# Perceiver layer on one core: Wv and Wo of the last cross-attention group multiplied beforehand, and the end of cross-attention reordered

## The reference, cut to what matters

```
x = x + xattn(layernorm(x), ctx)     # 16 heads over 8 K/V groups; x is 2 x 128 x 256, ctx is 2 x 2048 x 128
x = x + attn(layernorm(x))           # causal, 16 query heads, 4 groups
x = x + ffn(layernorm(x))            # 16 routed experts, top 2, and one shared
def xattn(h, c):
    q = h @ Wq;  k = c @ Wk;  v = c @ Wv
    attn = softmax(q @ k.T / sqrt(128))
    return (attn @ v) @ Wo
```

## Time and profile before

| | us |
|---|---|
| median of 3 executions | 351.37 (351.33 to 351.54) |
| the profiled execution, its own time | 349.24 |
| its span in the trace | 347.5 |
| TensorE busy in the span | 331.4 (95%) |
| DVE, ACT, POOL busy | 271.0, 232.4, 236.1 |

### The profile page before, as it was taken

One profiled execution on the slowest core, in us unless ns is written; L12 is line 12 of the kernel. 1 busy time (PEld: TensorE's weight loads), 2 busy tenths in 40 slices (PEclk: granted clock), 3 DMA queues, 4 the chain that ended last, 5 costly groups with the idle time before them and its releaser, 6 DMA issues.

```text
span 347.5 us, 6872 instructions
## 1 busy us (share of the span) xinstructions
PE 331.4 (95%) x2246; PEld 299.8 (86%) x2246; DVE 271.0 (78%) x469; ACT 232.4 (67%) x415; POOL 236.1 (68%) x146
## 2 busy tenths in 40 slices
PE   6899989999999999999999998999899999999995
PEld 5788868898999999999999987999798897698995
DVE  3787788897988988989889887754559745579997
ACT  3789467667687687777767775975355686266761
POOL 4593728798599599499598596859626768507650
PEclk9999999999999999999999999999999999999999
DMA  6811468776886895895795887890232040404630
GB/s 199 249 32 38 100 153 189 196 176 152 220 189 144 204 204 127 208 208 125 178 204 117 201 181 183 208 321 31 87 101 83 2 151 1 144 9 124 179 107 31
DMA packets 32566, 49.98 MB, mean 144 GB/s; under 512 B 5537, under 2 KB 23073, under 8 KB 32545
## 3 DMA queue, kind: packets, MB, share of 16 engines
q1 hardware_dynamic: 32544, 49.72, 56.6%
HBM read 20.08 MB, written 0.26 MB: 59 GB/s over the span
## 4 chain that ended last, share of the span: by engine, by line
PE 71%; DVE 9%; POOL 6%; issue 4%; ACT 4%; SPq 3%; DMA 2%; DVEq 0%; POOLq 0%; ACTq 0%
PE bank L573 10%; PE pair L573 10%; PE bank L574 10%; PE bank L575 10%; PE pair L574 10%; PE pair L575 10%; POOL pT L431 4%; SPq L272 3%; PE bank L717 2%; PE bank L876 1%; DMA ctx_raw<-in_ctx_dram 1%; DVE ctx_raw L1495 1%; PE bank L709 1%; PE pair L869 1%; DMA pT<-blocks 1%
## 5 line engine op out<-in xcount | busy, mean ns | idle before, releaser
L431 POOL TENSOR_TENSOR pT<-pT,pT_hi 128x1024 fp32r<-128x1024 f32 x56 | 133.4, 2407 | 35.3 <-ACT pT_hi L1135 35.3
L1125 ACT ACTIVATE probs<-probs,lowest 128x2048 f32<-128x2048 f32 x32 | 64.3, 2009 | 26.5 <-DVE lowest L1484 26.4
L1135 ACT ACTIVATE pT_hi<-pT 128x1024 fp32r<-128x1024 f32 x56 | 57.6, 1053 | 16.1 <-DMA pT<-ctx_raw 10.5
L573 PE MATMUL bank<-pT_hi,ctx_lo 128*128 128x256 f32 x224 | 63.8, 285 | 0.4 <-POOL pT L431 0.4
L574 PE MATMUL bank<-pT,ctx_hi 128*128 128x256 f32 x224 | 64.1, 286 | 0.0
L575 PE MATMUL bank<-pT_hi,ctx_hi 128*128 128x256 f32 x224 | 63.6, 284 | 0.0
L573 PE MATMUL pair<-ctxT_hi,qk_lo 128*128 128x512 f32 x128 | 52.1, 407 | 2.4 <-DVE lowest L1484 2.0
L575 PE MATMUL pair<-ctxT_hi,qk_hi 128*128 128x512 f32 x128 | 50.1, 391 | 0.0
L574 PE MATMUL pair<-ctxT_lo,qk_hi 128*128 128x512 f32 x128 | 50.1, 391 | 0.0
L1484 DVE CUSTOM_DVE_ANT_0 probs<-pair,mask_bias,lowest 128x1024 f32<-128x1024 f32 x32 | 41.0, 1281 | 9.3 <-PE pair L575 8.5
L431 POOL TENSOR_TENSOR ctx_lo<-ctx_raw,ctx_hi 128x512 fp32r<-128x512 f32 (+1 forms) x19 | 31.5, 1671 | 21.8 <-DVE route L1817 9.4
(11 more groups left out here) (253 smaller groups left out, 841.3 us busy)
## 6 DMA issues: line engine op xcount, KB each, us to landing
pT<-blocks SPq DMA_DIRECT2D x112, 128.0 KB, 2.3
pT<-ctx_raw SPq DMA_DIRECT2D x112, 128.0 KB, 2.3
ctx_raw<-ffn_experts_gate_up_dram SPq DMA_DIRECT2D x16, 256.0 KB, 2.8
wq<-in_L_xattn_Wq_dram SPq DMA_DIRECT2D x8, 256.0 KB, 2.6
ctx_raw<-in_ctx_dram SPq DMA_DIRECT2D x8, 256.0 KB, 6.4
wo<-in_L_xattn_Wo_dram SPq DMA_DIRECT2D x8, 256.0 KB, 2.8
blocks<-in_L_attn_w_dense_dram SPq DMA_DIRECT2D x4, 512.0 KB, 4.6
ctx_raw<-_L_ffn_experts_down_dram SPq DMA_DIRECT2D x16, 128.0 KB, 2.4
```

Of the source, the lines that this page charges most:

```text
L431: pool.tensor_tensor(dst, src, hi.bitcast(F32), ALU.subtract).then_inc(ready, 1)
L573: pe.matmul(dst, w[1], x[0], start=start, stop=False)
L1125: act.activation(probs[:, j], probs[:, j], ACT.Exp, bias=lowest[:, p, j, 1:2], scale=-1.0, accum_out=den[:, p, j:j + 1]).then_inc(exps, 1)
L1135: act.activation(hi_slot(c), chunk(p, c).bitcast(F32), ACT.Copy).then_inc(pT_hi_ready, 1)
```

## The change

For the last group alone, y_project and its round trip are removed: Wv and Wo are multiplied with each other beforehand. TensorE transposes Wv (`v_turn`), ACT copies it into wk, TensorE multiplies it with both halves of Wo in one plain float32 matmul (`vo_product`), ACT rounds the product into wq_hi and DVE makes wq_lo; `vo_project` then takes o straight to the output. `o_round(7)` and `rest_o(7)` are gone.

Further: in the last group ACT's oT_unit stands ahead of the first two p_rounds. Of the last unit's four low parts POOL makes those of chunks 0 and 2, DVE those of 1 and 3 (`odd_rest`). The last unit's attention is cut in blocks (`attend_blocks`) and spread around vo_project(14) and the transposes of batch 0. ACT rounds the query weights before oT of unit 14, and splits xnT before oT of unit 15. `scores2(0, 0)` comes before the transposes of batch 1, with two warm-up matmuls on either side of these in place of one, and the first query of batch 1 begins with the matmuls that need only the high part (`first_query`).

```diff
                 beats(g, True)
             for g in range(G - 2, G):
                 beats(g, False)
-            rest_o(G - 1)
-            for c in range(4):
+            for c in (0, 2):
                 rest_p(LAST - 1, 0, c)
             def split_q(r):
...
                                    (hi_block(c, i), lo_block(p, blk)), blk == 0, blk == NBLK - 1)
                 last.then_inc(av, 1)
+            def attend_blocks(first, end):
+                dst = O_BANK[0].rearrange("p (j q t) -> p j q t", j=J, q=QD)
+                for blk in range(first, end):
+                    c, i = blk // 4, blk % 4
+                    if i == 0 and c % 2 == 0:
+                        pe.wait_ge(pT_lo_ready, 4 * (LAST - 2) + c // 2 + 1)
+                    if i == 0 and c % 2 == 1:
+                        pe.wait_ge(odd_lo_ready, c // 2 + 1)
+                    last = product(dst, (ctx_hi[:, 0, blk], ctx_lo[:, 0, blk]), (hi_block(c, i), lo_block(0, blk)),
+                                   blk == 0, blk == NBLK - 1)
+                    if i == 3:
+                        last.then_inc(av, 1)
             def y_project(n, g):
-                w = (wkT_hi, wkT_lo) if isinstance(g, int) and g == G - 1 else (wv_hi, wv_lo)
                 pe.wait_ge(wv_ready, g + 1)
                 pe.wait_ge(oT_ready, n + 1)
                 after(pe, added, 2 * n)
-                product(YO_BANK[:, 0:J * T], (w[0][:], w[1][:]), (oT_hi[:], oT_lo[:]),
+                product(YO_BANK[:, 0:J * T], (wv_hi[:], wv_lo[:]), (oT_hi[:], oT_lo[:]),
                         True, True).then_inc(y_psum, 1)
             def out_project(n, g):
-                w = (wq_hi, wq_lo) if isinstance(g, int) and g == G - 1 else (wo_hi, wo_lo)
                 pe.wait_ge(wo_ready, g + 1)
                 pe.wait_ge(yT_ready, n + 1)
                 for j in range(J):
                     rows = slice(j * T, (j + 1) * T)
                     last = product(YO_BANK[:, j * H:(j + 1) * H], (yT_hi[:, rows], yT_lo[:, rows]),
-                                   (w[0][:, j], w[1][:, j]), True, True)
+                                   (wo_hi[:, j], wo_lo[:, j]), True, True)
+                last.then_inc(out_psum, 1)
+            def v_turn():
+                pe.wait_ge(ld_wv, 16 * G)
+                pe.wait_ge(masked, NB)
+                pe.transpose(bank[2][:, 0:P], wv[:], ident[:]).then_inc(vo_psum, 1)
+            def vo_product():
+                pe.wait_ge(vT_ready, 1)
+                pe.wait_ge(ld_wo, 16 * G)
+                pe.matmul(bank[2][:], wk[:], wo[:].rearrange("p j n -> p (j n)"), start=True, stop=True
+                          ).then_inc(vo_psum, 1)
+            def vo_project(n):
+                pe.wait_ge(vo_ready, 1)
+                pe.wait_ge(oT_ready, n + 1)
+                pe.wait_ge(added, 2 * n)
+                for j in range(J):
+                    rows = slice(j * T, (j + 1) * T)
+                    last = product(YO_BANK[:, j * H:(j + 1) * H], (oT_hi[:, rows], oT_lo[:, rows]),
+                                   (wq_hi[:, j], wq_lo[:, j]), True, True)
                 last.then_inc(out_psum, 1)
             def beat(g, m, fold_on, out_on, y_on):
...
                 if h == 1:
                     last.then_inc(done, 1)
+            def first_query(head, cols):
+                dst, (_, hi, lo) = QA[:, cols], wq2_of[0]
+                at = [slice((k * HR + head) * P, (k * HR + head + 1) * P) for k in range(HB)]
+                for k in range(HB):
+                    pe.matmul(dst, lo[:, at[k]], xnT_hi[:, k, cols], start=(k == 0), stop=False)
+                    pe.matmul(dst, hi[:, at[k]], xnT_hi[:, k, cols], start=False, stop=False)
+                pe.wait_ge(xnT_ready, 2 * B)
+                for k in range(HB):
+                    pe.matmul(dst, hi[:, at[k]], xnT_lo[:, k, cols], start=False, stop=(k == HB - 1))
             def queries2(r, cols):
                 pe.wait_ge(wq2_ready, r + 1)
                 for head in range(HR):
...
             both, of = slice(0, B * T), [slice(b * T, (b + 1) * T) for b in range(B)]
             for f in range(4, 8):
                 turn_final(f)
+            v_turn()
             attend(LAST - 2, 1, 3)
-            for c in range(2):
-                attend_final(c)
+            attend_final(0)
             y_project(LAST - 2, G - 2)
-            for c in range(2, 4):
-                attend_final(c)
+            vo_product()
+            attend_final(1)
             out_project(LAST - 2, G - 2)
-            attend(LAST - 1, 0, 0)
-            y_project(LAST - 1, G - 1)
-            attend(LAST - 1, 0, 1)
-            out_project(LAST - 1, G - 1)
-            attend(LAST - 1, 0, 2)
-            attend(LAST - 1, 0, 3)
+            attend_final(2)
+            attend_final(3)
+            attend_blocks(0, 3)
+            vo_project(LAST - 1)
+            attend_blocks(3, 12)
             xn_transpose(0, 1, WQK_BANK)
-            y_project(LAST, G - 1)
+            attend_blocks(12, NBLK)
             pe.wait_ge(xnT_ready, B + 1)
             pe.wait_ge(wq2_ready, 1)
             query(0, 0, of[0], first_q)
             query(0, 1, of[0], first_q)
-            out_project(LAST, G - 1)
+            vo_project(LAST)
             query(0, 2, of[0], first_q)
             query(0, 3, of[0], first_q)
             keys_values2(0, of[0], first_kv)
-            xn_transpose(1, 1, WQK_BANK)
-            keep_warm(bank[4], 1)
             pe.wait_ge(first_qk_ready, 2)
             scores2(0, 0)
-            pe.wait_ge(xnT_ready, 2 * B)
-            query(0, 0, of[1], qa_psum)
+            keep_warm(bank[4], 2)
+            xn_transpose(1, 1, WQK_BANK)
+            keep_warm(bank[4], 2)
+            pe.wait_ge(xnT_hi_ready, 2 * B)
+            first_query(0, of[1])
             query(0, 1, of[1], qa_psum)
             keys_values2(0, of[1], kv2_psum)
             query(0, 2, of[1], qb_psum)
...
             def o_round(g):
-                if isinstance(g, int) and g == G - 1:
-                    act.wait_ge(qk_psum, G)
-                    v, o = wkT_hi, wq_hi
-                else:
-                    after(act, out_psum, 2 * g)
-                    v, o = wv_hi, wo_hi
+                after(act, out_psum, 2 * g)
                 act.wait_ge(ld_wv, 16 * (g + 1))
-                act.activation(v[:], wv[:], ACT.Copy).then_inc(wv_hi_ready, 1)
+                act.activation(wv_hi[:], wv[:], ACT.Copy).then_inc(wv_hi_ready, 1)
                 act.wait_ge(ld_wo, 16 * (g + 1))
-                act.activation(o[:], wo[:], ACT.Copy).then_inc(wo_hi_ready, 1)
+                act.activation(wo_hi[:], wo[:], ACT.Copy).then_inc(wo_hi_ready, 1)
             def exp_row(g, row):
                 p, j = row // J, row % J
...
                     wq_round(g + 2)
                 exp_row(g, 1)
                 o_round(g - 1)
+                if last:
+                    oT_unit(2 * (g - 1), 0)
                 p_round(g - 1, 1, 0)
                 p_round(g - 1, 1, 1)
-                oT_unit(2 * (g - 1), 0)
+                if not last:
+                    oT_unit(2 * (g - 1), 0)
                 p_round(g - 1, 1, 2)
                 if fold_on:
                     fold_copy(g + 1, 0)
...
                 group(g, True, True, True)
             group(G - 2, False, True, True)
             group(G - 1, False, False, True, last=True)
-            o_round(G - 1)
             final_hi(0)
             final_hi(1)
             exp_row(G - 1, 3)
             for f in range(2, 8):
                 final_hi(f)
+            act.wait_ge(vo_psum, 1)
+            act.activation(wk[:], bank[2][:, 0:P], ACT.Copy).then_inc(vT_ready, 1)
             p_round(G - 1, 0, 0)
             oT_unit(LAST - 2, 1)
             p_round(G - 1, 0, 1)
             yT_copy(LAST - 2)
+            act.wait_ge(vo_psum, 2)
+            act.activation(wq_hi[:].rearrange("p k e -> p (k e)"), bank[2][:], ACT.Copy).then_inc(vo_hi_ready, 1)
             p_round(G - 1, 0, 2)
             p_round(G - 1, 0, 3)
+            act.wait_ge(ld_wq2[0], 16)
+            act.wait_ge(final_av, 2)
+            act.activation(wq2_hi, wq2, ACT.Copy).then_inc(wq2_hi_ready, 1)
             oT_copy(LAST - 1, O_FINAL, 1, final_av, 4)
-            act.wait_ge(ld_wq2[0], 16)
-            act.activation(wq2_hi, wq2, ACT.Copy).then_inc(wq2_hi_ready, 1)
             act.wait_ge(ld_wkv2, 32)
             act.activation(wk2_hi, wk2, ACT.Copy).then_inc(wk2_hi_ready, 1)
             act.activation(wv2, wv2_raw, ACT.Copy).then_inc(wv2_ready, 1)
-            yT_copy(LAST - 1)
             act.wait_ge(ld_wd2, 16)
             act.activation(wd2_hi, wd2, ACT.Copy).then_inc(wd2_hi_ready, 1)
             act.wait_ge(ld_wq2[1], 16)
...
                     if r == R - 1:
                         copy_c(r, b)
+            xnT_rows = xnT_copy(0, 1, WQK_BANK)
             oT_unit(LAST - 1, 0)
-            xnT_rows = xnT_copy(0, 1, WQK_BANK)
-            yT_copy(LAST)
```

(14 more changed lines are left out.)

8 lines of the change are left out of this document (4 added, 4 removed).

## The result

The changed kernel took **348.47 us** (median of four executions, 348.28 to 349.09) against 351.35 (351.15 to 351.54) for the kernel before beside it: a ratio of 0.9931, 95% interval 0.9911 to 0.9952. Forecast were 350.1 and a range from 349.1. So the direction was right, and the gain more than twice as large (2.9 against 1.3).

The account below looks back on a forecast made before the run. The stage was taken as bound by TensorE's own work plus few idle holes. Terms -1.05 - 0.85 + 0.6 gave -1.3 us: 347.9 for the profiled execution, 350.1 with the offset to the median unchanged; range 349.1 to 351.9.

Parts of the forecast that it names:

- its offset to the median: Last step: the profiled execution of before, 349.24, against its median, 351.37; the difference was assumed equal for the changed kernel.
- Part 1: Last group: ACT makes oT of unit 12 ahead of two roundings, so y_project(12) need not wait; 1.05 us earlier.
- first mark: TensorE's first matmul of the last quarter of unit 13's attention, 227.41 before; forecast shift -1.05 us.
- Part 2: Unit 13's attention to batch 0's first query: two y_projects removed, Wv x Wo added, smaller holes; -0.85 us.
- first two marks: From unit 13's last attention quarter (227.41) to the first query of batch 0 (245.08), 17.67 us before.
- Part 3: First query of batch 0 to that of batch 1: scores ahead of transposes give back 0.6 us.
- Rival 1: POOL keeps its turn, DVE's low part waits, vo_project(14) has a hole of 3.1 us; 352.5 us, chance 0.13.
- Rival 2: Nothing measurable: slower DVE low parts or a later key copy enlarge hole and give-back; 351.0 us, chance 0.16.
- Rival 3: More gain: DVE and POOL don't meet, and scores fit under the wait for the rows; 349.1 us, chance 0.12.

Follow-up runs that it names:

- before_again: The kernel before, unchanged, measured again: 350.22 us, ratio 0.9978 to before.
- after_early_filled: The changed kernel with only the early wait of TensorE filled, by nine warm-up matmuls: 347.58 us, ratio 0.9928 to before.
- after_scores_behind: The changed kernel with batch 0's scores again behind batch 1's transposes, one warm-up matmul, the first query in its old order: 347.64 us, ratio 0.9925 to before.
- only_scores_first: The kernel before with only batch 0's scores ahead of batch 1's transposes, four warm-up matmuls, first query begun with high parts: 351.89 us, ratio 1.0012.

## Why the prediction was wrong, and where it was right

**The step that failed** is the last of the sum: "its offset to the median, 351.37, is taken as unchanged". For the changed kernel that offset measured 0.2 (348.47 less 348.28), not 2.1. The sum is then 349.24 less the 1.0 between the two profiled executions, plus 0.2. The offset of 2.1 us was not something around the execution. What is shown of it is TensorE's time at the 1.2 GHz level, in two places, each behind a wait: the early stretch leaves 0.7 to 0.9 us, the late one 1.18 in its one trace, together about the 1.95 between the outer clusters, and filling both waits takes 1.1 off the median. The profiled execution happened to have neither (the clock is 1.00 in the earlier trace rows as in all its stretches up to 345). The first three executions of before, 351.33 to 351.54, lie at the median of the cluster at 0.990 or less, 351.49, but their clocks are not on record. A second cause is seen in single traces: a late start, 1.30 us in before_again and 2.06 in after_early_filled. How much of the first 2.1 it made up is open. A median made of such executions doesn't carry over to a kernel with other waits. Part 1 ends the wait for DVE's addition; of the changed kernel's 15 executions none is at 0.990 or less, of before's 83 there are 26.

The hint was on the page: three executions within 0.2 of each other, all 2.1 to 2.3 above the profiled one. I carried the difference over instead of asking what it was.

**Part 1** (-1.05 at the first mark) was right where the blocks land no later than in the trace of before: -0.96 (226.45). In the changed kernel's own trace it was -0.20, since the blocks landed 0.8 later; that varies from execution to execution in either order. Medians at full clock make part 1 worth 0.6, but of three and four executions.

**Part 2** (-0.85) came out at -1.17 (16.50 us between the first two marks, and 16.51 in after_scores_behind, against 17.67). The product cost 0.86 (230.53 to 231.51 with one matmul of 0.12 in between), not 0.77. The hole before vo_project(14) is about 0.4, not 0.7: DVE's second low part was shut out by POOL as expected and took 2.25, but oT_lo still started only 0.16 behind the end of oT_hi. The Trainium skill (SBUF — State Buffer, section Who interferes with whom) has the two engines exclude each other; the trace agrees, 2.25 against 1.22, and 3.10 against 2.4 on POOL's side. (The row that the prediction gave for it, 2.44 against 0.28, was of a copy with one input; this one has both its inputs in SBUF.) That the parts on DVE also clear POOL ahead of rstd, worth 0.6 (at full clock, four executions of each kernel; the transposes' wait is 0.77), was missing in my sum.

**Part 3** (+0.6) came out at +0.65 in the traces and 0.7 at full clock. It made the kernel slower, and 0.37 of that are two warm-up matmuls. In after_scores_behind and its old order the parts add up to -0.96 - 1.17 + 0.65 = -1.48 for the change, against -1.3: part 2's surplus more than makes up for what parts 1 and 3 fell short.

**The rivals.** Rival 1 (POOL keeps its turn) did not come: DVE's low part ended at 237.40 inside POOL's pair of instructions, which took 4.07 instead of 3.1. Rival 2 did not come either. Rival 3's time, 349.1, is nearer than the forecast's, but not by its mechanism: DVE and POOL did meet, and the scores did not fit. At equal clock the forecast came within 0.1 to 0.5 of the medians, with intervals of about 1 us.

**Not settled.** The clusters of the early stretch lie 1.2 us apart in the kernel before and 0.4 in the changed one (348.13 to 348.57), although the stretch costs both the same 0.7 to 0.9 in the traces. Of the six profiles with the stretch, the three of kernels made from before started 0.74 to 1.30 us later than the first profile of before, the three made from the changed kernel 0.25 early to 0.17 late, and executions with the late stretch alone fall into the same cluster; whether that holds for the executions without a profile no run tells. Nor does any trace show why the clock falls behind one and the same wait in one execution and not in the next. And before_again had no execution at 0.990 or less among 11, where the same code had 26 among 83; the share varies, so the counts of single kernels are weak evidence, and the filled waits with the traces that show the stretches in place are the strong part.

## What to carry to other kernels

When the profiled execution is faster than all the timed ones, find out what they lose before adding a forecast to their median; here it was TensorE's clock, which the mean clock of every single execution told, and a varying start, which it did not. A wait of TensorE costs more than its length if the clock falls behind it: filling two of them with matmuls into a free bank cost nothing that could be seen and gave 1.1 us between medians, and a reordering that removes the wait can gain more than the path says. And before giving work back to an in-order engine, look which small instruction stands behind it in the queue.

## What the runs showed of the hardware that was not expected

- TensorE's granted clock fell to the 1.2 GHz level behind waits of 1.96 us (in before_again, from about 55.2 to 58.6) and 2.29 us (in only_scores_first, 218.6 to 222.0). It did not fall behind the same waits, 1.96 and 1.64 us, in the first profile of before. The mean clock was under 0.998 in 57 of 83 executions of the kernel before, and full in the other 26, with the same program.
- A matmul of 512 columns follows the one ahead in 0.43 us there, in 0.23 at full clock; the early stretch costs 1.55 us at its own end and 0.7 to 0.9 at the y_project at 82 us, in both kernels, the late one 1.18 in its one trace.
- In after_early_filled matmuls of 256 columns followed each other at 0.21 us from about 9.5 to 11.6, while the clock column read 1.00; a mean clock of 1.00 did not tell of it.
- The same DMA of the blocks landed between 2.69 and 3.56 us behind the same POOL instruction, in kernels of either order.
